# Queries that keep their length, later keys scaled on GpSimd, and plane work one step sooner, in a two-block attention and expert kernel

## What is computed

```python
q = heads(_dwconv_silu(q_in, qconv_w))
k = heads(_dwconv_silu(k_in, kconv_w))
v = heads(_dwconv_silu(v_in, vconv_w))
q = q * jax.lax.rsqrt(jnp.sum(q * q, axis=-1, keepdims=True) + 1e-12)
k = k * jax.lax.rsqrt(jnp.sum(k * k, axis=-1, keepdims=True) + 1e-12)
...
def step(carry, x):
    vec, St = carry
    u, r, c, ca, sa, qt, kt, vt, at, bt = x
    ...
    vec_new = u * rot + r * c
    pred = jnp.einsum('bhij,bhi->bhj', St, kt)
    delta = vt - pred
    S_new = at[..., None, None] * St + bt[..., None, None] * (kt[..., :, None] * delta[..., None, :])
    read = jnp.einsum('bhij,bhi->bhj', S_new, qt)
    return ((vec_new, S_new), (vec_new, read))
...
m = _rmsnorm(reads, rms_m_w).reshape(b, s, D)     # over the 8 numbers of a head, eps 1e-6
```

## Time and profile before

| | us |
|---|---|
| median of 3 runs | 645.19 |
| lowest, highest | 644.34, 645.59 |
| the profiled execution, its own time | 645.17 |
| its span in the profile | 643.4 |
| granted TensorE clock, mean of the span | 0.944 of full speed |

### The profile page before, as it was taken

One profiled execution on the slowest core, in us unless ns is written; L12 is line 12 of the kernel. 1 busy time (PEld: TensorE's weight loads), 2 busy tenths in 40 slices (PEclk: granted clock), 3 DMA queues, 4 the chain that ended last, 5 costly groups with the idle time before them and its releaser, 6 DMA issues.

```text
span 643.4 us, 14314 instructions
## 1 busy us (share of the span) xinstructions
PE 565.3 (88%) x4610; PEld 479.6 (75%) x4610; DVE 467.9 (73%) x1372; ACT 429.7 (67%) x1037; POOL 383.1 (60%) x434
## 2 busy tenths in 40 slices
PE   2899999999999999899997689876965887798996
PEld 2788999689994999769995368654643755586785
DVE  7553468856677558864205799899999999996946
ACT  3266568556775568645686888978777887786543
POOL 5354046701574045725555313787999999998884
PEclk9999999999999999989999698777978987998999
DMA  8944652146412652134312000000000000000002
GB/s 279 336 180 57 188 115 61 51 55 171 84 58 53 143 105 58 53 58 80 71 47 89 0 1 2 2 2 0 1 1 2 0 2 0 2 2 1 3 2 67
DMA packets 104122, 39.85 MB, mean 62 GB/s; under 512 B 85906, under 2 KB 96178, under 8 KB 103922
## 3 DMA queue, kind: packets, MB, share of 16 engines
q1 hardware_dynamic: 98018, 29.34, 20.0%
q0 software_dynamic: 4480, 9.30, 4.3%
q10 hardware_dynamic: 1552, 0.30, 0.2%
HBM read 20.32 MB, written 18.59 MB: 60 GB/s over the span
## 4 chain that ended last, share of the span: by engine, by line
PE 52%; DVE 31%; ACT 8%; DMA 4%; issue 3%; POOL 2%; SPq 0%; DVEq 0%; POOLq 0%; ACTq 0%
PE PS L2359 17%; PE PS L2344 17%; DVE W2s L1414 4%; ACT W1s L1974 3%; DVE W1s L1559 2%; PE PS L2259 2%; DVE W1s L1528 2%; DVE PS L1552 2%; DMA rw<-in_L_ffn_routers_dram 2%; DVE PS L1530 2%; DVE PS L1532 2%; DVE PS L1534 2%; DVE W1s L1550 2%; DVE W1s L1562 2%; PE PS L2707 2%
## 5 line engine op out<-in xcount | busy, mean ns | idle before, releaser
L764 POOL DMA_INDIRECT sorted_x<-xrow,pos x93 | 90.4, 972 | 125.7 <-DVE pos L1227 99.1
L2359 PE MATMUL PS<-W2s,hbuf 128*128 x992 | 139.3, 284 | 0.0
L2344 PE MATMUL PS<-hbuf,swt 128*128 128x128 f32 x992 | 131.8, 276 | 1.0 <-DVE hbuf L1292 0.9
L2359 PEld LDWEIGHTS PS<-W2s,hbuf 128*128 128x128 f32 x992 | 126.7, 191 | 0.5
L2344 PEld LDWEIGHTS PS<-hbuf,swt 128*128 128x128 f32 x992 | 121.0, 192 | 1.7 <-DVE swt L1286 1.3
L1744 ACT ACTIVATE hbuf<-PS 128x512 f32<-128x512 f32 x124 | 73.2, 590 | 40.0 <-PE PS L2344 38.7
L1752 ACT ACTIVATE xrow<-PS,tags 128x144 f32<-128x144 f32 (+1 forms) x124 | 46.9, 378 | 42.0 <-PE PS L2359 39.8
L1974 ACT ACTIVATE W1s<-W1s,ab 128x128 f32<-128x128 f32 x168 | 51.3, 392 | 15.3 <-DVE W1s L1562 15.2
L2546 PE MATMUL PS<-ewT,xT 128*128 128x512 f32 x64 | 38.5, 733 | 21.0 <-ACT W2s L2025 21.0
L880 POOL TENSOR_TENSOR W1s<-W1s,kT 128x1024 f32<-128x1024 f32 x22 | 52.2, 2381 | 7.0 <-DVE W1s L1562 5.8
L1295 DVE STREAM_TRANSPOSE hbuf<-hbuf 128x128 f32<-128x128 f32 x116 | 33.4, 300 | 30.1 <-DMA hbuf<-sorted_x 29.6
(11 more groups left out here) (425 smaller groups left out, 1318.7 us busy)
## 6 DMA issues: line engine op xcount, KB each, us to landing
hbuf<-sorted_x SPq DMA_DIRECT2D x224, 32.0 KB
sorted_x<-slotbuf SPq DMA_DIRECT2D x9, 520.0 KB, 3.0
W1s<-in_L_ffn_W_dram SPq DMA_DIRECT2D x1, 4096.0 KB, 20.4
sorted_x<-slotbuf SPq DMA_DIRECT2D x1, 2015.0 KB, 12.0
sorted_x<-xrow,pos POOLq DMA_INDIRECT x109, 2.4
sorted_x<-slotbuf SPq DMA_DIRECT2D x3, 455.0 KB, 2.8
xres<-in_L_attn_x_dram SPq DMA_DIRECT2D x4, 256.0 KB, 4.6
xrow<-results SPq DMA_DIRECT2D x4, 256.0 KB, 4.0
```

The costliest lines, as they stand in the source:

```text
L764: pool.indirect_dma_start(xs_dram[l + 1][:, :], bass.IndirectOffsetOnAxis(ap=pos[:, t:t + 1], axis=0), xrow[:, t % NR, 0:XW], None).then_i ...
L2344: m = pe.matmul(PS[:, 2 + n, f * P:(f + 1) * P], w1st[:, (c - 1) % WB, f * P:(f + 1) * P], xring[:, (c - 1) % R, :], start=True, stop=True)
L2359: m = pe.matmul(PS[:, 4 + n, 0:w], hTs[:, n, f * P:(f + 1) * P], W2s[:, f * YW:f * YW + (E - 1) * NF + w][:, bass.ds(w2, w)], start=(f == ...
```

## The change

Queries are no longer divided by their length. Instead each read's mean square gets a term that stands for the eps: ACT squares all queries at once (2048 numbers per partition, step 2), PE sums them by head with 16 matmuls (step 3), ACT scales the sums by 1e-6 into `query_eps` (step 4), and `mean_squares` adds them by a matmul with the identity. With that its own matmuls move 16 columns instead of 128.

Keys from step 4 on are divided by their length once, on POOL, in one product of 1792 numbers per partition behind `bKc`; `next_keys` then only copies them to PSUM. The first four are still multiplied in `next_keys`.

ACT's `plane`, `value`, `update_plane` and `keep_plane`, PE's `chunks` and `plane`, and POOL's `plane_summed`, `plane_scaled` and `plane_kept` all move one step earlier, and `vec_step` begins at `VEC_AT` = 7, spread over 20 steps. It ends in the same step as before.

```diff
@@ -135,8 +135,10 @@
     SELT_AT = 6
-    VEC_AT = 8
-    VSTEPS = C - 13
+    QUERY_EPS_AT = 4
+    SQUARES_OF_Q = 2
+    VEC_AT = 7
+    VSTEPS = C - 12
     VPER = 4
...
@@ -272,12 +274,14 @@
         eps_kq = sb("eps_kq", [P, 1])
+        eps_q = sb("eps_q", [P, 1])
         eps_log = sb("eps_log", [P, 1])
...
         ab = sb("ab", [P, C, 2 * HP])
-        nstd = wraw[:, :, :].rearrange("p n d -> p (n d)").rearrange("p (n m) -> p n m", n=2)
+        nstd = wraw[:, 0:2, :].rearrange("p n d -> p (n d)")
+        query_eps = wraw[:, 2:4, :].rearrange("p n d -> p (n d)")
         scratch = plane_tmp[:, :]
...
@@ -845,22 +850,22 @@
             pool.tensor_tensor(cosp, cosp, cosp, ALU.mult).then_inc(cos_ready, 1)
-            squared_lengths(0)
+            squared_lengths()
             pool.wait_ge(ab_ready, 1)
...
             binv = abraw[:, :, 0:HP]
-            step(pool.tensor_tensor(binv, ab[:, :, HP:2 * HP], nstd[:, 0, :].rearrange("p (t h) -> p t h", t=C), ALU.mult))
+            step(pool.tensor_tensor(binv, ab[:, :, HP:2 * HP], nstd.rearrange("p (t h) -> p t h", t=C), ALU.mult))
             for tt in (slice(0, KB), slice(KB, C)):
...
                                    ALU.mult).then_inc(bk_ready, 1)
-            squared_lengths(1)
+            pool.wait_ge(bk_ready, 2)
+            pool.tensor_tensor(Kc[:, KB:C, :, :], Kc[:, KB:C, :, :],
+                               nstd.rearrange("p (t h) -> p t h", t=C)[:, KB:C, :].unsqueeze(3).to_broadcast([P, C - KB, HP, HD]),
+                               ALU.mult).then_inc(bk_ready, 1)
             plane_summed(0)
-            pool.wait_ge(unit_ready, 2)
-            q_all = Qc.rearrange("p t h i -> p (t h) i")
-            step(pool.tensor_tensor(q_all, q_all, nstd[:, 1, :].unsqueeze(2).to_broadcast([P, C * HP, HD]), ALU.mult))
...
@@ -875,22 +880,24 @@
                 pool.wait_ge(x_new, 2 * (t + 1))
+                if t % (C // NG) == 0:
+                    pool.wait_ge(pa_ev, JOB_EV[f"q{t // (C // NG)}"])
                 if t >= QR:
...
                 if t < VEC_AT:
-                    if t == 2:
+                    if t == 1:
                         plane_summed(1)
-                    elif t == 4:
+                    elif t == 3:
                         plane_scaled(0, 0)
                         plane_scaled(0, 1)
+                    elif t == 4:
+                        plane_kept(0)
                     elif t == 5:
-                        plane_kept(0)
-                    elif t == 6:
                         plane_scaled(1, 0)
                         plane_scaled(1, 1)
-                    elif t == 7:
+                    elif t == 6:
                         plane_kept(1)
...
@@ -1447,20 +1454,22 @@
-            def unit(n):
-
-                dve.wait_ge(len_ready, 2 * n + 2)
-                dve.reciprocal(nstd[:, n, :], nstd[:, n, :]).then_inc(unit_ready, 1)
-                dve.wait_ge(unit_ready, n + 1)
+            def key_scales():
+
+                dve.wait_ge(len_ready, 2)
+                dve.reciprocal(nstd, nstd).then_inc(unit_ready, 1)
+                dve.wait_ge(unit_ready, 1)
...
                 k = keys.rearrange("p t h i -> p (t h) i")
+                if t:
+                    return mark(dve.tensor_copy(keys.rearrange("p t h i -> p (t h i)"), Kc[:, t:t + KB, :, :].rearrange("p t h i -> p (t h i)")))
                 return mark(dve.tensor_tensor(k, Kc[:, t:t + KB, :, :].rearrange("p t h i -> p (t h) i"),
-                                              nstd[:, 0, t * HP:(t + KB) * HP].unsqueeze(2).to_broadcast([P, KB * HP, HD]), ALU.mult))
+                                              nstd[:, t * HP:(t + KB) * HP].unsqueeze(2).to_broadcast([P, KB * HP, HD]), ALU.mult))
...
             turn_plane(3)
-            unit(0)
+            key_scales()
             dve.wait_ge(pa_ev, JOB_EV["q0"])
...
@@ -1535,8 +1544,8 @@
                     pred_r = mark(dve.tensor_tensor(pred[:, R_, :], pred[:, R_, :], v, ALU.subtract))
-                if t == KB - 1:
-                    dve.wait_ge(bk_ready, 2)
+                if t in (ROUTE_AT, KB - 1):
+                    dve.wait_ge(bk_ready, 2 if t == ROUTE_AT else 3)
                 if t == ROUTE_AT:
...
@@ -1560,8 +1569,6 @@
                 dve.tensor_tensor(xn[:, R_, :, :], aX[:, R_, :, :], outer[1], ALU.subtract).then_inc(x_new, 1)
-                if t == 1:
-                    unit(1)
...
@@ -1896,7 +1903,8 @@
                 o = bank()
-                act.activation(squares_of[n][:, g * 512:(g + 1) * 512], o, ACT.Square).then_inc(sq_ready, 1)
+                if n == 0:
+                    act.activation(key_squares[:, g * 512:(g + 1) * 512], o, ACT.Square).then_inc(sq_ready, 1)
                 act.activation(dst[:, g * SB:(g + 1) * SB, :, :].rearrange("p t h i -> p (t h i)"), o, ACT.Copy).then_inc(pa_ev, 1)
...
@@ -1956,15 +1964,15 @@
-            def lengths(n):
-                act.wait_ge(len_ready, 2 * n + 1)
-                act.activation(nstd[:, n, :], nstd[:, n, :], ACT.Sqrt, bias=eps_kq[:, 0:1]).then_inc(len_ready, 1)
+            def key_lengths():
+                act.wait_ge(len_ready, 1)
+                act.activation(nstd, nstd, ACT.Sqrt, bias=eps_kq[:, 0:1]).then_inc(len_ready, 1)
...
-            lengths(0)
+            key_lengths()
             chunked(1, Qc, 0)
...
@@ -2038,21 +2046,24 @@
                     reads_evac(t // G - 1)
-                if t == 1:
-                    lengths(1)
-                if t in (2, 3):
-                    value(t - 1)
+                if t == SQUARES_OF_Q:
+                    act.activation(query_squares[:, :], post[1], ACT.Square).then_inc(sq_ready, 1)
                 if t in (1, 2):
-                    plane(zpl[:, t - 1, :], ACT.Silu, pbias[:, 1 + t:2 + t])
+                    value(t)
+                if t in (0, 1):
+                    plane(zpl[:, t, :], ACT.Silu, pbias[:, 2 + t:3 + t])
                 if t == ROUTE_AT + 1:
...
                     act.activation(lg1[:, 2, :, :], lg1[:, 1, :, :], ACT.Tanh, scale=0.5).then_inc(ex1, 1)
+                if t == QUERY_EPS_AT:
+                    act.wait_ge(pd_mm, 6)
+                    act.activation(query_eps, PS[:, 1, 0:NT * H], ACT.Identity, scale=1e-6, bias=eps_q[:, 0:1]).then_inc(len_ready, 1)
                 if t == SELT_AT:
...
                     act.activation(selT, PS[:, 1, :], ACT.Copy).then_inc(selT_ev, 1)
-                if 3 <= t < 7:
-                    (update_plane if t % 2 else keep_plane)((t - 3) // 2)
-                if t == 4:
+                if 2 <= t < 6:
+                    (keep_plane if t % 2 else update_plane)((t - 2) // 2)
+                if t == 3:
                     value(3)
...
@@ -2601,11 +2611,18 @@
             for t in range(C):
-                if t in (3, 4):
-                    chunks(2, (t - 1,))
-                if t in (2, 3, 5):
-                    plane({2: OFF[2] + 1, 3: OFF[0], 5: OFF[0] + 1}[t], 2)
+                if t in (2, 3):
+                    chunks(2, (t,))
+                if t in (1, 2, 4):
+                    plane({1: OFF[2] + 1, 2: OFF[0], 4: OFF[0] + 1}[t], 2)
+                if t == QUERY_EPS_AT - 1:
+                    pe.wait_ge(sq_ready, NG + 1)
+                    pe.wait_ge(sh1, 1)
+                    for n in range(NT):
+                        m = pe.matmul(PS[:, 1, n * H:(n + 1) * H], query_squares[:, n * P:(n + 1) * P], headsel[:, :], start=True, stop=True)
+                    m.then_inc(pd_mm, 1)
                 if t == SELT_AT - 1:
+                    pe.wait_ge(len_ready, 3)
                     pe.wait_ge(sel_ready, 1)
...
@@ -2655,12 +2672,10 @@
                 pe.wait_ge(osq_ready, n + 1)
+                pe.matmul(PS[:, half, 0:G * H], ident[:, :], query_eps[:, half * G * H:(half + 1) * G * H], start=True, stop=False)
                 for t in range(G):
                     tt = half * G + t
-                    r = P // H
-                    m = pe.matmul(PS[:, half, t * H:(t + r) * H].rearrange("p (r h) -> p r h", r=r),
-                                  osq[:, tt * P:(tt + 1) * P], headmean[:, :].unsqueeze(1).to_broadcast([P, r, H]),
-                                  start=True, stop=True)
+                    m = pe.matmul(PS[:, half, t * H:(t + 1) * H], osq[:, tt * P:(tt + 1) * P], headmean[:, :], start=False, stop=(t == G - 1))
                 m.then_inc(oms_mm, 1)
```

16 lines of the change are left out of this document (8 added, 8 removed).

## The result

| | before | changed |
|---|---|---|
| median us | 644.94 | 651.6 |
| lowest, highest | 644.34, 645.59 | 649.54, 652.88 |
| the profiled execution, its own time | 645.17 | 650.07 |
| its span, mean granted clock | 643.4, 0.944 | 648.3, 0.939 |

The medians are of five executions each; the 645.19 of the kernel before that stands further up is the median of three of them. The change makes the kernel slower: the ratio is 1.0085, 95% interval 1.0064 to 1.0106, which is +4.1 to +6.8 us. The forecast was 648.4 with 644.0 to 650.2, a loss of 3.2 us. The sign was right, but the loss was about twice as large (6.7 us by the medians, 5.5 by the ratio), and the median lies outside the range.

What follows compares the result with a forecast made beforehand. It took DVE's 32 recurrence steps (404 to 582 us) as the bound, then PE up to 630 us. +1.42 - 0.96 + 3.6 = +4.05 at step 4, -0.8 behind: +3.2 on 645.17 gives 648.4 us, range 644.0 to 650.2.

Steps and rivals of the forecast that it cites:

- `choose2` beside `plane_scaled`: Step 4: POOL's two products hold up DVE's two-input operations, the largest loss; step 4's first subtraction +4.05 us.
- The price of the place alone: Step 4: choose2 takes 7.6 us against 4.0 beside POOL's products, +3.6 us; bounds -0.64 and +4.2.
- the 0.64: Step 4: lower bound of choose2's term, -0.64 us, if no operation waits, not even where one did before.
- (a): Step 4: choose2 isn't held up by plane_scaled, -0.64 rather than +3.6, total 644.2 us; chance alone 0.12.
- (c): Step 4: only one of the two plane_scaled holds DVE up, -2.1 us, total 646.3; chance 0.08.
- ACT in step 3: Recurrence: squares, table load and plane in step 2 make ACT's decayed state late for step 3, +1.42 us.
- (b): Step 3: ACT isn't late, shift -0.35 rather than +1.42 us, total 646.6; chance alone 0.07.
- The copies: next_keys on DVE: 0.42 us each without waiting for POOL, gaining 0.96 at step 3 and 1.02 later.
- PE's 32 passes for the queries' sums: Step 3 on PE: 3.74 us of passes while PE waits for ACT and DVE, costing 0.
- Behind step 4: Later recurrence steps: -0.1 us where ACT was late in step 7, and -1.02 from the keys.
- The end: mean_squares on PE: 10 passes at 0.117 us, four times +0.08, +0.3 us; bounds -0.5 and +0.6.
- (d): PE drops to its lower clock in one more step with experts, +1.8 us, total 650.2; chance 0.09.

Runs made afterwards that it cites:

- e1: Changed kernel with all of POOL's plane work put back to its earlier steps, narrow calls kept; median 648.72 us, ratio 1.0059 to the kernel before.
- e12: Changed kernel with ACT's squares of the queries in step 4 instead of step 2; median 647.86 us, ratio 1.0043 to the kernel before.
- e7: Kernel before with only the keys part: POOL scales keys from step 4 on in one product, next_keys copies them; ratio 0.9954 to the kernel before.
- e9: Changed kernel with all four mean_squares wide, the queries' eps kept; median 699.04 us on the slower chip, ratio 1.0062 to the kernel before.
- e14: Changed kernel with three 128-column matmuls filling PE's pause ahead of mean_squares of call 2, narrow passes kept; ratio 1.006 to the kernel before.
- e11: Changed kernel unaltered, run a third time for spread and profile; median 651.19 us, ratio 1.008 to the kernel before.
- e13: The kernel of e1 again, for one profile: one execution, no ratio; recurrence end +0.00, 65.42 us behind it.
- e8: Changed kernel with POOL's plane work put back, squares in step 4 and all four mean_squares wide; ratio 0.9992 to the kernel before.
- e17: The kernel of e8 with calls 2 and 3 of mean_squares narrow; median 647.55 us, ratio 1.0017 to the kernel before.
- e15: The kernel of e7 with POOL's plane_summed(1) moved from step 2 to step 4, ahead of plane_scaled; ratio 0.9992 to the kernel before.
- e5: Changed kernel unaltered, run again on the slower chip; median 702.49 us, ratio 1.0117 to the kernel before.
- e10: The kernel of e8 again, beside the changed kernel and the one before on one chip; median 645.03 us, ratio 0.9992 to the kernel before.

## Why the prediction was right or wrong

- **The forecast for `choose2` beside `plane_scaled` held**: step 4 forecast at +4.05, measured +4.00. The two operations took 2.33 and 2.06 (2.4 and 2.2 were named). The price of the place alone, forecast +3.6 with `choose2` at 7.6, was 3.2 with `choose2` at 7.17; e1 took 3.87 off, which is this and the 0.64. Rivals (a) and (c) fall. The 0.4 too much come from two small things. The forecast let the second `plane_scaled` wait 0.3 us for `choose2`'s first operation; the two ran in 4.79 us without a gap. And it let the third operation end 0.29 us behind POOL's end; it ended 0.14 behind (436.64 and 436.50). A row of the kernel before had that already: of the two operations said to end 0.28 behind POOL's, that is so for L1459 (427.83 and 427.55), while L1492 ended at 432.69, 0.15 behind 432.54. The Trainium skill, "SBUF — State Buffer", section "Who interferes with whom", has the lock held for a whole instruction; e7's pair of rows agrees, 0.14 us apart.
- **ACT in step 3**: forecast +1.42, measured +1.78 (1.72 to 2.09 in the nine profiles with the squares in step 2). The squares took 1.90 as forecast. Step 1 stood at +1.62 rather than +1.28, and `decayed` of step 3 started at 423.75, which is 424.43 on the clock of the kernel before, against 424.1. e12 gives the squares 1.3. Rival (b) falls. The two errors, -0.4 in `choose2` and +0.4 here, cancelled in step 4: that it was hit to 0.05 us is luck, that both terms were there isn't.
- **The copies**: 0.42 each, as forecast. PE's 32 passes for the queries' sums took 3.75 us (3.74 named) and cost DVE nothing here. Behind step 4 the forecast was -1.1, measured -1.5 (4.00 to 2.51); the profiles of the changed kernel scatter by 0.7 here.
- **The end is the step that failed.** "Four times +0.08, on PE's path: +0.3", with bounds -0.5 and +0.6, priced the narrow passes by their number at an unchanged clock. By passes it is +0.5 (e9, e14). The other 2.6 us are the granted clock: 14.15 against 11.52. The prediction read passes of 8 columns at 0.117 us in a stretch whose granted clock was 1.00 (408 to 411 us), took that clock for the end as well, and never asked what 16 columns in place of 128 do to it. The clock term was put at nothing there, and that is the part that failed.
- **Rival (d)** had a fall of the clock in it, but at another place: a longer pause in step 5. That pause came (PE stood still for 6.10 us, up to 439.13), and the clock was at 0.50 from 437.2 to about 454, where in the kernel before it fell at 442.5. But DVE lost nothing by it: the shift is +4.00 in step 4, +3.91 in step 7, +3.68 in step 8 and never above +4.03 later. The loss came at the end of the kernel instead, which (d) doesn't name.
- **The range** ended at forecast plus (d), 650.2. With the end's term at 3.07 the sum is 2.5 + 3.1 = +5.6 against 645.17, 650.8; the ratio gives +5.5. The medians differ by 6.7; the last 1.1 is not in the first profile. The third one (e11, 651.17 us, at its group's median) has +3.21 in the recurrence and +3.08 behind it, 6.3 together, so part of it is the recurrence's scatter; the rest stays open.

## What to carry to other kernels

A matmul's width can be what keeps TensorE at 2.4 GHz: before cutting 128 columns to 16 near a pause, price the work behind it at both levels. Keep such passes wide, or try to fill the pause where they can't be (one profile here stands for that). When work moves to an earlier step of another engine, look for two-input vector operations that it will now lie beside; here two products of 2.4 us each cost the other engine 3.2 us, and no profile shows a cost of putting them back. Profiles of one kernel mostly agree in a step to a few tenths where single times scatter by 5 us, so attribute by stages. But take more than one profile: e1 and e13, one kernel, end the recurrence 1.3 us apart, as do e8 and e17, which are alike up to there. And a gain in one stage may be waited away in the next, as in e7 and e15.

## What the runs showed of the hardware that was not expected

- PE can be recorded as busy for 100% of a stretch while its clock goes down: e1 from 619 to 633 us, +6.7 us, begun in passes of 16 columns and carried on through passes of 128.
- The same kernel does it in one execution and not in another: e1 and e13 are 6.6 us apart in the scan, while the changed kernel's own three profiles are alike to 0.03 us in the last two calls. The Trainium skill, "TensorE: Matmul & The Clock Gate", "Part 1: The HAM clock gate (the "warmup" mystery)", says that where a change of clock falls varies from run to run for one kernel. The traces agree that the place varies, and go further: whether a fall comes at all varies too.
- Eight narrow passes and eight wide ones take nearly the same at 2.4 GHz: 1.02 us (e14) and 1.11 (e9's last call), so little was to be won by narrowing.
- On one of the chips the recurrence began 46 to 52 us later for each of the four kernels run there, while the recurrence and what is behind it took the same to some 0.2 us in the pairs that compare (changed and e5, e8 and e10).
- In the pause of 4.15 us ahead of the queries' sums in e17 the clock went to 0.50, and it stayed there through 32 passes of 16 columns and more, 13.6 us in all; the one late gate cost DVE 1.22 us two steps on.
